# A selective state-space layer with routed experts on one core: state product, state-out product and turned decay sums at other places in the engines' queues

## The chip, the cores and the metric

One core of one Trainium2 chip. The metric is the device time of one execution in microseconds. Before: median 832.32 of 3 runs (832.04 to 833.04).

## The reference, cut to what matters

The input is 16 sequences of 512 tokens with 128 features, float32. Two layers follow one another, each with a residual and a layer norm.

```
# layer 1, for each sequence (4 heads of 64, 128 states)
z, xBC, dt = split(x @ Win.T)                 # 256, 512, 4 columns
xBC = silu(causal_conv4(xBC) + conv_b)        # x_ssm 256, B 128, C 128
dtp = softplus(dt + dt_bias); dA = exp(dtp * A)
h_t = dA_t * h_(t-1) + (dtp_t x_t) B_t        # per head
y_t = C_t . h_t + D x_t
x = layernorm(x + (rmsnorm(y) * norm_w * silu(z)) @ Wout.T)
# layer 2: 8 experts, the 2 best by sigmoid gate for each token
x = layernorm(x + sum of gate * (gelu(x @ W1[e] + b1[e]) @ W2[e] + b2[e]))
```

## The kernel before, in words

The recurrence is computed by chunks of 128 tokens, four to a sequence. Inside a chunk it is a masked matrix: exponents of differences of running sums (`exponents`, line 408, bank `pl`), exponentiated by ACT (`exp_exponents`, 681, into `L`), multiplied with the inner products of B and C by DVE (`mask_chunk`, 973, tile `M`), and applied to the inputs `Xdt` on PE (line 535, bank `p7`). Across chunks it is a state of 128 x 256: the **state product** B^T Xdd (line 549, bank `p6`, right half) gives what a chunk adds; DVE copies it (line 1102) or adds the decayed old state (1105) into `state`; PE multiplies C with the state (the **state-out product**, line 517, `p6`, left half); DVE scales that to `carried` (1075); PE adds it to `p7` (541); DVE adds the skip part to get `yv` (1097); ACT squares it (`square`, 779). POOL makes `Xdd` from `Xdt` (`decay_x`, 1351), `decayed` from `state` (`decay_state`, 1346), and the gated product (`gate_y`, 1329). `Xdt` itself is made by DVE (1069) out of PE's transposes (511, 513) in bank `p5`, after ACT has copied the transposed B out of the same bank to `Btok` (797).

Every engine has a queue written out by hand. The loop over slots (`slots`, 308) has in slot s three sequences at work: sequence s is scanned (`s`), sequence s+1 is projected (`q`), sequence s-1 is normalised and routed (`r`); DVE and POOL finish the ranks and scatters of sequence s-2. A slot has four chunks c = 0 to 3 on PE, ACT and DVE, and a part behind them. In chunk c the projection of block c of the next sequence runs as well: a product (`project_block`, 388, bank `pj`), tap 0 on ACT (`tap0`, 722), taps 1 to 3 on DVE (`tap`, 910; those of block c-1 stand in chunk c, tap 1 at its head and taps 2 and 3 ahead of `yv`; those of block 3 behind the chunks). After the chunks PE runs `z_block` 0 (396), which waits until the taps of blocks 0, 1 and 2 are done because it writes the bank of block 2, then the sums of squares (584, waiting for all four squares), the output product (592), `inner_products` (483) and `z_block` 1.

In chunk 1 PE also turns the split running sums of the next sequence (`turn_parts`, 404, bank `p4`), ACT copies them to `S` (`keep_parts`, 716) for the next slot's exponents, and, behind four normalisations (`rowA`, 805), PE transposes the normalised rows (559) into the same bank `p4`. The bank also holds the ranks of sequence s-2 until DVE has read them (`take_ranks`, 983, at the end of chunk 0, ending with `next_row`, 990). So `turn_parts` has a wait ahead of it:

```
if route:
    wait(pe, rank_read, r.n)      # r.n = s - 1: the ranks that DVE reads in this slot
turn_parts(q, p4[0:KS, 0:P])
```

The order of PE in chunk c is: exponents of c+1, transposes of c, state-out product of c, projection block c, (chunk 1: `turn_parts`), masked product and `carried` of c, state product of c, (chunk 1: 559; chunk 2: gate logits, 574). The order of DVE is: tap 1, `Xdt`, (chunk 0: statistics), `carried`, (chunk 1: `shift`), `mask_chunk` of c+1, taps 2 and 3, `yv`, `state`, (chunk 0: ranks; chunk 1: `place_rows`, 993). Slot 0 has no `route` part and splits the decay sums of all further sequences; slot 15 has no `project` part. After slot 16 a table of tiles is made, the experts run over 136 tiles of rows, and a last loop adds and normalises.

## Time and profile before

| | |
|---|---|
| Median of 3 runs | 832.32 us |
| The profiled execution's own time | 836.54 us |
| Its span, first to last instruction | 834.7 us |
| Mean granted TensorE clock | 0.934 |
| Entering all sequences | 0 to about 55 us |
| Slots 0 to 15 | about 55 to 464 us |
| One slot of 2 to 14 | 25.6 us |

Busy time is given by engine (PE matmuls, PEld weight loads, DVE, ACT, POOL), times from the span's start. In a timeline a line stands for neighbouring instructions of one source line; matmuls are pipelined, so that a row's start is the issue of the first and its duration runs to the modelled end of the last, and rows may overlap. In brackets stands the idle time of the engine before the row, and what ended it. PEclk 1.00 is a granted clock of 2.4 GHz, half of it 1.2 GHz.

### The profile page before, as it was taken

The page shows a single profiled execution, that of the slowest core. Times are in us where ns is not written, and L with a number is a line of the kernel's source. Part 1 is how long each engine was busy: PE and PEld are TensorE (multiplying, and loading weights), DVE is VectorE, ACT ScalarE, POOL GpSimd, SP SyncE. Part 2 cuts the span into 40 slices and gives each one's busy share as a digit, 9 for nine tenths or more (in the row PEclk, how much of TensorE's full clock was granted, in tenths as well). Part 3 has the DMA queues.
Part 4 walks back from the last instruction along what each step waited for, and adds up shares of the span by engine and source line. Part 5 has one row for each costly group of instructions (what it writes and reads, how often), then busy time and mean ns, then how long its engine had stood idle before and what let it go on. Part 6 is the DMA issues. An engine that isn't in the chain of part 4 may idle for free.

```text
span 834.7 us, 21104 instructions
## 1 busy us (share of the span) xinstructions
PE 678.3 (81%) x5092; PEld 552.6 (66%) x5093; DVE 623.1 (75%) x2142; ACT 475.0 (57%) x1179; POOL 435.5 (52%) x498
## 2 busy tenths in 40 slices
PE   6859998998888998889987319999999999989300
PEld 4736565666556665656665309999999999989300
DVE  3457898999999899998996455667667666657485
ACT  2535667676676666676765106555555555546265
POOL 3002345755656656566656653555555555545464
PEclk9979999999999999999999759999999999999755
DMA  9070001110111101111100122222222222222397
GB/s 253 1 252 1 14 17 36 39 36 17 33 33 39 39 17 37 30 36 39 29 24 21 36 74 55 65 67 64 63 62 68 64 61 66 66 57 65 104 297 210
DMA packets 74801, 54.09 MB, mean 65 GB/s; under 512 B 9435, under 2 KB 70110, under 8 KB 74480
## 3 DMA queue, kind: packets, MB, share of 16 engines
q1 hardware_dynamic: 56400, 31.90, 14.5%
q0 software_dynamic: 8448, 16.93, 6.1%
q10 hardware_dynamic: 9888, 4.49, 1.9%
q8 instruction: 29, 0.48, 0.2%
q14 instruction: 36, 0.29, 0.1%
HBM read 31.11 MB, written 22.69 MB: 64 GB/s over the span
## 4 chain that ended last, share of the span: by engine, by line
PE 68%; issue 9%; ACT 8%; DVE 8%; POOL 3%; DMA 2%; ACTq 1%; SPq 1%; DVEq 0%; POOLq 0%
PE pl L628 15%; PE p L640 14%; PE pj L393 4%; PE p L535 3%; PE p L584 3%; PE p L592 3%; PE p L541 2%; PE pj L622 2%; ACT rowA L805 2%; ACT sz L869 2%; POOL sorted_rows L1341 2%; PE p L549 2%; PE p L517 2%; PE pl L419 2%; PE pl L414 2%
## 5 line engine op out<-in xcount | busy, mean ns | idle before, releaser
L848 ACT ACTIVATE L<-pl,b_sb 128x128 f32<-128x128 f32 x544 | 154.9, 368 | 121.7 <-PE pl L628 117.0
L1403 POOL DMA_INDIRECT moe_rows<-yv,xs x136 | 147.3, 1083 | 142.1 <-issue 92.9
L628 PE MATMUL pl<-Btok,M 128*128 128x128 f32 x1088 | 152.5, 284 | 2.4 <-DVE M L1198 2.2
L917 DVE SCALAR_TENSOR_TENSOR acc<-pj,conv_w_sb,acc 128x511 f32<-128x511 f32 (+2 forms) x192 | 142.8, 744 | 4.6 <-ACT acc L725 1.7
L640 PE MATMUL p<-w,L 128*128 x1088 | 144.8, 276 | 1.3 <-ACT L L848 1.3
L628 PEld LDWEIGHTS pl<-Btok,M 128*128 128x128 f32 x1088 | 134.4, 194 | 5.8 <-DVE M L1198 2.5
L640 PEld LDWEIGHTS p<-w,L 128*128 128x128 f32 x1088 | 133.2, 193 | 1.8 <-issue 1.8
L1194 DVE COPY Btok<-pj 128x128 f32<-128x128 f32 x136 | 39.7, 292 | 78.3 <-PE pl L628 63.8
L1354 POOL TENSOR_TENSOR Xdd<-Xdt,cur 128x256 f32<-128x256 f32 x48 | 29.6, 616 | 102.7 <-DVE Xdt L1069 94.4
L1341 POOL DMA_INDIRECT sorted_rows<-rowA,slot x64 | 64.7, 1011 | 19.2 <-issue 17.1
L1341 POOL DMA_INDIRECT sorted_rows<-rowB,slot x64 | 62.7, 979 | 18.0 <-issue 18.0
L393 PE MATMUL pj<-xT,w_xbc 128*128 128x512 f32 x128 | 69.4, 627 | 1.4 <-DVE acc L917 1.4
L725 ACT ACTIVATE acc<-pj,conv_b_sb,conv_w_sb 128x512 f32<-128x512 f32 x64 | 49.3, 772 | 31.7 <-PE pj L393 31.7
L535 PEld LDWEIGHTS p<-M,Xdt 128*64 128x64 f32 x512 | 27.7, 138 | 57.5 <-issue 44.9
L683 ACT ACTIVATE pl<-pl 128x512 f32<-128x512 f32 x64 | 37.3, 582 | 43.5 <-PE pl L419 42.8
L622 PE MATMUL pj<-ident,xs 128*128 128x128 f32 x136 | 40.1, 295 | 23.3 <-DMA xs<-sorted_rows 20.8
L1198 DVE COPY M<-w 128x512 f32 x136 | 56.9, 419 | 0.0
L1334 POOL TENSOR_TENSOR gt<-yv,sz 128x256 f32<-128x256 f32 x64 | 46.9, 733 | 13.5 <-DVE yv L1097 12.8
L535 PE MATMUL p<-M,Xdt 128*64 128x128 f32 x512 | 42.8, 287 | 13.6 <-DVE Xdt L1069 11.4
L1207 DVE TENSOR_TENSOR yv<-p,b2e_mem 128x128 f32<-128x128 f32 x136 | 39.6, 291 | 18.5 <-PE p L640 9.8
L1210 DVE SCALAR_TENSOR_TENSOR yv<-yv,xs 128x128 f32<-128x128 f32 x136 | 47.9, 352 | 4.8
L979 DVE TENSOR_TENSOR M<-pl,Gm 128x512 f32<-128x512 f32 x64 | 43.8, 685 | 0.6
(205 smaller groups left out, 1355.2 us busy)
## 6 DMA issues: line engine op xcount, KB each, us to landing
xs<-sorted_rows SPq DMA_DIRECT2D x136, 65.0 KB
xres<-in_x SPq DMA_DIRECT2D x16, 256.0 KB
w<-in_w SPq DMA_DIRECT2D x2, 2048.0 KB, 9.8
acc<-moe_rows SPq DMA_DIRECT2D x16, 256.0 KB, 4.1
xc<-moe_rows SPq DMA_DIRECT2D x16, 256.0 KB, 4.9
out<-sz ACTq DMA_DIRECT2D x16, 256.0 KB, 4.8
moe_rows<-yv,xs POOLq DMA_INDIRECT x136
xc<-in_x SPq DMA_DIRECT2D x4, 256.0 KB, 4.7
```

The costliest lines, as they stand in the source:

```text
L393: pe.matmul(pj[k % 2][:, :], w_xbc[:, k * P:(k + 1) * P], xT[:, q.n, :], start=True, stop=True).then_inc(proj_psum, 1)
L535: mm = pe.matmul(p7[half, (h // 2) * P:(h // 2 + 1) * P], Xdt[c % 2][:, h * HD:(h + 1) * HD], M[c % 2][:, h, :], start=(h < 2), stop=(c == ...
L622: pe.transpose(pj[k % 2][:, 0:P], xs[k][:, 0:P], ident[:, :]).then_inc(sT_psum, 1)
L628: mm = pe.matmul(pl[k % 2][:, f * P:(f + 1) * P], w1e[k % 2][:, f * P:(f + 1) * P], sT[k % 2][:, :], start=True, stop=True)
L640: mm = pe.matmul(o[:, 0:P], hT[k % 2][:, f, :], w2[:, bass.ds(e, 1), f, :].rearrange("p e d -> p (e d)"), start=(f == 0), stop=(f == FB - 1))
L725: act.activation(acc[:, c, :], pj[c % 2][:, :], ACT.Identity, bias=conv_b[:, c:c + 1], scale=conv_w[:, c, TAPS - 1:TAPS]).then_inc(tap0_do ...
L848: act.activation(hT[k % 2][:, f, :], pl[k % 2][:, f * P:(f + 1) * P], ACT.Gelu, bias=b1[:, bass.ds(e * FB + f, 1)]).then_inc(hT_ready, 1)
L917: ins = dve.scalar_tensor_tensor(out=acc[:, k, j:TOKS], in0=pj[k % 2][:, 0:TOKS - j], scalar=conv_w[:, k, TAPS - 1 - j:TAPS - j], in1=acc[ ...
L1198: dve.tensor_copy(w1e[k % 2], w1[:, bass.ds(e, 1), :].rearrange("p e f -> p (e f)")).then_inc(w1e_ready, 1)
L1210: dve.scalar_tensor_tensor(out=ye[k % 4], in0=ye[k % 4], scalar=xs[k][:, P + 1:P + 2], in1=xs[k][:, 0:P], op0=ALU.mult, op1=ALU.add).then_ ...
L1341: pool.indirect_dma_start(out=sorted_rows[:, :], out_offset=bass.IndirectOffsetOnAxis(slot[q.par][:, c, k:k + 1], 0), in_=(rowA, rowB)[k][ ...
L1403: pool.indirect_dma_start(out=moe_rows[:, :], out_offset=bass.IndirectOffsetOnAxis(xs[k][:, P:P + 1].bitcast(I32), 0), in_=ye[k % 4], in_o ...
```

## The change

On PE the state product of chunk c-1 no longer closes chunk c-1 but stands in chunk c behind the exponents of c+1 and the transposes of c. The state-out product of c stands behind projection block c instead of ahead of it. `turn_parts`, with its waits, stands behind the exponents of chunk 1, ahead of the transposes. On ACT the copy to `S` stands at the head of chunk 1, ahead of the copy to `Btok`, and `set_current` stands in chunk 3. On DVE `state` of c-1 stands behind `Xdt` of c, and `carried` behind `mask_chunk` of c+1. On POOL `decay_x` of chunks 1 and 2 stands ahead of `decay_state` of the same chunk.

```diff
--- before.py
+++ after.py
@@ -502,6 +502,13 @@
                         if not route and c == 0:
                             pe.wait_ge(v_ready, 2)
                         exponents(s if c + 1 < NC else q, (c + 1) % NC)
+                    if project and c == 1:
+                        if q.n == G0:
+                            pe.wait_ge(parts_ready, 2)
+                            pe.wait_ge(decays_ready, 3)
+                        if route:
+                            wait(pe, rank_read, r.n)
+                        turn_parts(q, p4[0:KS, 0:P])
                     if scan:
                         pe.wait_ge(Xdt_ready, n) if not isinstance(n, int) or n > 0 else None
                         wait(pe, Btok_ready, (NC - 1) * s.n + c)
@@ -512,19 +519,20 @@
                         if c + 1 < NC:
                             mm = pe.transpose(p5[:, CC * P:(CC + 1) * P], xc[s.par][:, CC, tok], ident[:, :])
                         mm.then_inc(tr_psum, 1)
-                        if c > 0:
-                            pe.wait_ge(state_ready, (NC - 1) * s.n + c)
-                            pe.matmul(p6[:, 0:DI], xc[s.par][:, CC + 1, tok], state[(c - 1) % 2][:, :],
-                                      start=True, stop=True).then_inc(off_psum, 1)
+                    if scan and c > 0:
+                        k = c - 1
+                        pe.wait_ge(Btok_ready, (NC - 1) * s.n + c)
+                        pe.wait_ge(Xdd_ready, (NC - 1) * s.n + c)
+                        if k == 0:
+                            pe.wait_ge(sz_ready, CC * (s.n + 1))
+                        pe.matmul(p6[:, DI:2 * DI], Btok[k % 2][:, :], Xdd[k % 2][:, :],
+                                  start=True, stop=True).then_inc(state_psum, 1)
                     if project:
                         project_block(q, c)
-                    if project and c == 1:
-                        if q.n == G0:
-                            pe.wait_ge(parts_ready, 2)
-                            pe.wait_ge(decays_ready, 3)
-                        if route:
-                            wait(pe, rank_read, r.n)
-                        turn_parts(q, p4[0:KS, 0:P])
+                    if scan and c > 0:
+                        pe.wait_ge(state_ready, (NC - 1) * s.n + c)
+                        pe.matmul(p6[:, 0:DI], xc[s.par][:, CC + 1, tok], state[(c - 1) % 2][:, :],
+                                  start=True, stop=True).then_inc(off_psum, 1)
                     if scan:
                         pe.wait_ge(M_ready, n + 1)
                         pe.wait_ge(Xdt_ready, n + 1)
@@ -541,13 +549,6 @@
                                 mm = pe.matmul(p7[:, k * P:(k + 1) * P], carried[:, k * P:(k + 1) * P],
                                                ident[:, :], start=False, stop=True, skip_group_check=True)
                         mm.then_inc(y_psum, 1)
-                        if c + 1 < NC:
-                            pe.wait_ge(Btok_ready, (NC - 1) * s.n + c + 1)
-                            pe.wait_ge(Xdd_ready, (NC - 1) * s.n + c + 1)
-                            if c == 0:
-                                pe.wait_ge(sz_ready, CC * (s.n + 1))
-                            pe.matmul(p6[:, DI:2 * DI], Btok[c % 2][:, :], Xdd[c % 2][:, :],
-                                      start=True, stop=True).then_inc(state_psum, 1)
                     if route and c == 1:
                         pe.wait_ge(u_ready, NC * (r.n + 1))
                         wait(pe, rank_read, r.n)
@@ -791,6 +792,8 @@
                     n = NC * s.n + c
                     if scan and c > 0 and (c + 1 < NC or project):
                         exp_exponents(n + 1, c + 1)
+                    if project and c == 1:
+                        keep_parts(q, p4[0:KS, 0:P])
                     if scan and c + 1 < NC:
                         act.wait_ge(tr_psum, n + 1)
                         wait(act, state_psum, (NC - 1) * s.n + c - 1)
@@ -806,15 +809,14 @@
                                            bias=shift[:, k:k + 1], scale=rstd[:, k:k + 1]).then_inc(u_ready, 1)
                     if project:
                         tap0(q, c)
-                    if project and c == 1:
-                        set_current(q)
-                        keep_parts(q, p4[0:KS, 0:P])
                     if not route and c == 2:
                         decay(2, G0, SEQS, 2, 4)
                     if not route and c == 3:
                         decay(3, G0, SEQS, 4, 5)
                     if scan and c > 0:
                         square(s, c - 1)
+                    if project and c == 3:
+                        set_current(q)
                     if route and c == 1:
                         act.wait_ge(u_ready, NC * (r.n + 1))
                         act.wait_ge(uT_psum, r.n + 1)
@@ -1071,10 +1073,14 @@
                     if route and c == 0:
                         statistics(r)
                     if scan and c > 0:
-                        dve.wait_ge(off_psum, (NC - 1) * s.n + c)
-                        dve.tensor_tensor(heads(carried[:, :]), heads(p6[:, 0:DI]),
-                                          per_head(cur[s.par][:, 2, :], c),
-                                          ALU.mult).then_inc(carried_ready, 1)
+                        k = c - 1
+                        dve.wait_ge(state_psum, (NC - 1) * s.n + c)
+                        if k == 0:
+                            dve.tensor_copy(state[0][:, :], p6[:, DI:2 * DI]).then_inc(state_ready, 1)
+                        else:
+                            dve.wait_ge(decayed_ready, (NC - 2) * s.n + k)
+                            dve.tensor_tensor(state[k % 2][:, :], p6[:, DI:2 * DI], decayed[:, :],
+                                              ALU.add).then_inc(state_ready, 1)
                     if route and c == 1:
 
                         dve.wait_ge(rstd_ready, r.n + 1)
@@ -1083,6 +1089,11 @@
                                                  op1=ALU.mult).then_inc(shift_ready, 1)
                     if scan and c + 1 < NC:
                         mask_chunk(s, c + 1)
+                    if scan and c > 0:
+                        dve.wait_ge(off_psum, (NC - 1) * s.n + c)
+                        dve.tensor_tensor(heads(carried[:, :]), heads(p6[:, 0:DI]),
+                                          per_head(cur[s.par][:, 2, :], c),
+                                          ALU.mult).then_inc(carried_ready, 1)
                     if not route and c == 2:
                         split(1, G0, SEQS)
                     if project and c > 0:
@@ -1096,14 +1107,6 @@
                         wait(dve, g_ready, n - 1)
                         dve.tensor_tensor(yv[c % 2][:, :, :], p7[:, 0:DI].rearrange("p (k d) -> p k d", k=CC),
                                           xD[s.par][:, :, c * P:(c + 1) * P], ALU.add).then_inc(yv_ready, 1)
-                    if scan and c + 1 < NC:
-                        dve.wait_ge(state_psum, (NC - 1) * s.n + c + 1)
-                        if c == 0:
-                            dve.tensor_copy(state[0][:, :], p6[:, DI:2 * DI]).then_inc(state_ready, 1)
-                        else:
-                            dve.wait_ge(decayed_ready, (NC - 2) * s.n + c)
-                            dve.tensor_tensor(state[c % 2][:, :], p6[:, DI:2 * DI], decayed[:, :],
-                                              ALU.add).then_inc(state_ready, 1)
                     if c == 0 and not (isinstance(s.n, int) and s.n < 2):
                         take_ranks(s.plus(-2))
                     if c == 1 and not (isinstance(s.n, int) and s.n < 2):
@@ -1368,11 +1371,11 @@
                     pool.wait_ge(ve_ready, r.n + 1)
                     pool.tensor_tensor(rstd[:, :], ve[:, :], neg_half[:, :], ALU.pow).then_inc(rstd_ready, 1)
                 if scan:
+                    decay_x(s, 1)
                     decay_state(s, 1)
-                    decay_x(s, 1)
                     gate_y(s, 0)
+                    decay_x(s, 2)
                     decay_state(s, 2)
-                    decay_x(s, 2)
                     gate_y(s, 1)
                 if scatters:
                     scatter(old, 0, 0)
```

## Rows read from the trace of the kernel before

**Rows 1.** Windows of 25.6 us: slots 7 and 15.
```profile
core 0: us, PE busy (x) PEld busy (x) DVE busy (x) ACT busy (x) POOL busy (x), PEclk, DMA share, GB/s
...
236.40:262.00 25.60, 22.70 (x162) 15.85 (x161) 23.03 (x75) 17.50 (x35) 15.87 (x20) 1.00 0.11 32
...
441.20:466.80 25.60, 17.75 (x134) 13.29 (x131) 16.32 (x74) 8.31 (x19) 17.32 (x21) 0.93 0.08 25
```

**Rows 2.** Timeline of PE, slot 7, chunks 0 to 2 (start, duration, line, shapes, idle).
```profile
238.16 0.66 PE L535 MATMUL p<-M,Xdt 128*64 128x128 f32 x8 [0.18 <-DVE Xdt L1069]
240.06 0.67 PE L549 MATMUL p<-Xdd,Btok 128*128 128x256 f32 x2 [1.24 <-issue]
240.56 0.38 PE L414 MATMUL pl<-too_early,ident_b 128*128 128x512 bf16 x1
...
241.22 0.39 PE L511 MATMUL p<-ident,xc 128*128 128x128 f32 x2
...
241.99 1.02 PE L393 MATMUL pj<-xT,w_xbc 128*128 128x512 f32 x2
242.84 0.22 PE L406 MATMUL p<-ident_b,parts 128*96 128x128 bf16 x1
...
246.21 0.63 PE L559 MATMUL p<-ident,rowA 128*128 128x128 f32 x4 [1.48 <-ACT S L720]
```

**Rows 3.** Timeline of DVE, slot 7, chunks 0 to 2.
```profile
240.14 0.42 DVE L1097 TENSOR_TENSOR yv<-p,xD 128x256 f32<-128x256 f32 x1
240.76 0.42 DVE L1102 COPY state<-p 128x256 f32<-128x256 f32 x1 [0.20 <-PE p L549]
...
241.39 0.17 DVE L990 TENSOR_TENSOR next_row<-p,next_row 128x8 f32<-128x8 f32 x1
...
242.27 0.43 DVE L1069 TENSOR_TENSOR Xdt<-p,cur 128x256 f32<-128x256 f32 x1
...
242.94 0.46 DVE L1081 SCALAR_TENSOR_TENSOR shift<-mv,rstd 128x4 f32<-128x4 f32 x1
...
245.37 0.42 DVE L1097 TENSOR_TENSOR yv<-p,xD 128x256 f32<-128x256 f32 x1
...
247.23 0.74 DVE L917 SCALAR_TENSOR_TENSOR acc<-pj,conv_w_sb,acc 128x511 f32<-128x511 f32 x1
248.39 0.42 DVE L1069 TENSOR_TENSOR Xdt<-p,cur 128x256 f32<-128x256 f32 x1 [0.41 <-issue]
```

**Rows 4.** Timeline of ACT, slot 7, chunk 1.
```profile
241.91 0.27 ACT L797 COPY Btok<-p 128x128 f32<-128x128 f32 x1
243.44 1.65 ACT L805 ACTIVATE rowA<-rowA,shift,rstd 128x128 f32<-128x128 f32 x4 [1.26 <-DVE shift L1081]
...
245.81 0.26 ACT L720 CAST S<-p 96x128 bf16<-96x128 f32 x1
```

**Rows 5.** Timeline of PE, slot 7, chunk 3 and the start of what follows.
```profile
252.14 0.39 PE L511 MATMUL p<-ident,xc 128*128 128x128 f32 x2
...
252.80 1.02 PE L393 MATMUL pj<-xT,w_xbc 128*128 128x512 f32 x2
...
254.92 1.12 PE L401 MATMUL pj<-xT,w_z 128*128 128x512 f32 x2
256.01 2.02 PE L584 MATMUL p<-ones,ysq 128*128 128x96 f32 x16
```

**Rows 6.** Timeline of DVE, slot 7, chunk 3.
```profile
253.00 0.42 DVE L1075 TENSOR_TENSOR carried<-p,cur 128x256 f32<-128x256 f32 x1
253.34 1.52 DVE L917 SCALAR_TENSOR_TENSOR acc<-pj,conv_w_sb,acc 128x510 f32<-128x510 f32 x2
```

**Rows 7.** Timeline of PE: slot 0 (chunk 3), slot 1 (chunk 1), slot 15 (behind chunk 0).
```profile
74.17 1.91 PE L393 MATMUL pj<-xT,w_xbc 128*128 128x512 f32 x2
...
93.15 0.63 PE L559 MATMUL p<-ident,rowA 128*128 128x128 f32 x4 [1.12 <-issue]
...
444.92 1.03 PE L549 MATMUL p<-Xdd,Btok 128*128 128x256 f32 x2 [1.24 <-issue]
```

## The prediction

> **What bounds the kernel now.** I read first the windows, one per slot. The slots 2 to 14 are alike: 25.6 us, in slot 7 PE busy for 22.70 and DVE for 23.03 [rows 1]. Neither engine is full, both are nearly so, and a change of order can cost on one what it gives on the other. The second view is PE's timeline of slot 7. It shows two real holes: 1.24 us ahead of the state product, and 1.48 ahead of the transposes of the normalised rows, ended by ACT's copy to S [rows 2]. These are what the change aims at. With 0.18 ahead of the masked product they make up the 2.9 us that PE is idle. The third view is DVE's timeline: it hardly pauses; it waits 0.41 ahead of the third Xdt [rows 3]. The last is the fourth chunk on both: the z product (254.92) starts as soon as taps 2 and 3 of block 2 end (253.34 + 1.52 = 254.86) [rows 5, 6]. That place has no slack.
>
> **Chunk 0 into 1: the first hole stays, under another name.** I go through slot 7 at its own times. Until the masked product at 238.16 nothing differs. PE then has the exponents at once (0.66, from 240.56 to the transposes at 241.22), done near 239.4. But next comes `turn_parts` with its wait for `rank_read`. DVE gives that at the end of chunk 0, with `next_row`, and its queue up to there is bound by its own work: yv at 240.14. Before, `next_row` came 0.63 behind the start of the state copy (240.76 to 241.39) [rows 3]; that copy is gone from there and yv (of the same duration) stands in its place, so `next_row` starts at 240.77 and ends at 240.94. PE turns the parts at 241.05, 0.11 behind it (S ends at 246.07 and its waiter starts at 246.21, 0.14 behind) [rows 2, 4]. The transposes of chunk 1 come 0.1 later, at 241.15, where they were at 241.22. So PE waits about 1.5 us at `turn_parts` instead of 1.24 at the state product. On ACT, exponents and S copy now lie ahead and done, so Btok follows the transposes at 241.75 instead of 241.91 [rows 4], and Xdt comes at 242.11 instead of 242.27. The state copy stands where `carried` stood, both 0.42, so `shift` comes at 242.79 and the row normalisation at 243.29, 0.15 sooner.
>
> **The second hole closes.** The transposes of the rows no longer wait for S, only for the rows: 243.29 + 1.65 + 0.14 = 245.08, against 246.21 [rows 2, 4]: 1.13 sooner.
>
> **But carried and the taps behind it come later.** The state-out product now stands behind the projection (0.85, 241.99 to 242.84) [rows 2] and waits for the state copy, ready at 242.87: it starts at 243.0 and ends at 243.6. DVE works from Xdt to yv without a pause, 3.10 us before (242.27 to 245.37) and 0.33 more with the state copy among it: yv comes at 242.11 + 3.43 = 245.54, 0.17 later [rows 3]. Carried, with taps 2 and 3 behind it (some 1.77), starts at 243.77 and just doesn't wait. The state add behind yv (0.33) is gone, so the next tap 1 comes 1.53 behind yv (1.86 before, 245.37 to 247.23), at 247.07, and the third Xdt at 247.87, since Btok is there before it: 0.52 sooner than 248.39 [rows 3]. In chunk 2 the state add ends at 248.63; PE has finished projection 2 at 247.83 and waits 0.9 for it: a new hole. State-out at 248.75, carried 0.64 behind it at 249.39, yv at 251.17 (before, 251.09). The gate logits and exponents behind it end at X = 252.02 instead of 252.14 [rows 5]. So of 1.13 us only 0.12 reach the fourth chunk.
>
> **Chunk 3: the price.** Before, from X: carried at X + 0.86, then the taps of block 2 (0.34 behind, 1.52 long), and the z product at X + 2.78 [rows 5, 6]. Now a state product (0.44) and the projection (0.85) are ahead of the state-out product. The 0.44 is read so: three transposes and one state-out product take 0.77 (241.22 to 241.99), two and one take 0.66 (252.14 to 252.80), so a transpose takes 0.11 and a 128x256 product 0.44 [rows 2, 5]. DVE has nothing to do in place of the wait, since the taps 2 and 3 are queued behind carried. Carried comes at X + 0.86 + 0.44 + 0.85 = X + 2.15, the taps end at X + 2.15 + 0.34 + 1.52 = X + 4.01, the z product starts at X + 4.13: 256.15, 1.23 later. The sums of squares started 1.09 behind it, since they waited for the last square; now the square is done in time and they start 0.87 behind it: 257.02 against 256.01. From there to the end of the slot PE works without a hole (z, squares, output, inner products), and everything moves by **1.01 us a slot**. What else moved is covered: `set_current` (0.25) on ACT lies in that engine's free time in chunk 3; POOL gets Xdt sooner than it can use it, and Xdd (0.61) is wanted by nobody until the next chunk. No DMA is added.
>
> **Sum.** Slots 2 to 14: 13 x 1.01 = +13.1. Slot 1 has no ranks to wait for: `turn_parts` runs at once, and by the same count the rows' transposes come at 91.93, right behind carried, instead of 93.15 [rows 7], 1.22 sooner; no `place_rows` is ahead of the third Xdt either, so more of it lasts, some 0.76 at the fourth chunk, and the tail takes 1.13: +0.4. Slot 0 runs partly at half clock (a projection of 1.91 us against 1.02) [rows 2, 7] and starts its second chunk's exponents a cold state product (about 1.0) sooner; I take -1.5, with ends 0 and -3. Slot 15 has no z product and no taps: it loses the 1.24 us wait [rows 7] and its `turn_parts` is absent, so its second chunk gains some 2.5, and chunks 2 and 3 lose 1.0 and 1.1 for the state add between two products of PE: -0.4, ends -2 and +1. Together +11.6. The profiled execution took 836.54 us and would take 848.1; it lies 4.2 above the median of 832.32, so as a median: **844**.
>
> **Rivals.** *A small loss* (13%): DVE's ranks come sooner than I count, or the hole of chunk 2 is smaller, and all slots behave as slot 1: 14 x 0.4 - 1.9 = +3.7, 836. For it: DVE's pauses are inferred from dense rows. Against: yv at 240.14 is queue-bound.
>
> *Faster* (7%): both holes close and the z product has slack after all, because taps 2 and 3 of block 2 don't depend on the chain through the projection. PE would save 1.24 + 1.48 and pay only the 1.29 us by which carried is later: -1.43 a slot, -20 over 14 slots, 812. It decides at the start of the fourth chunk's transposes: from X - 1.1 on the change pays. Against it: `turn_parts` can't pass `rank_read`, and `carried` is ahead of the taps in DVE's queue.
>
> *A clock drop* (13%). In slot 15 PE is idle for 1.04, works 0.66, is idle for 1.24, and the state product then takes 1.03 where it took 0.67 in slot 7: 1.2 GHz instead of 2.4; the slot's mean is 0.93 [rows 2, 1, 7]. The new slot has 0.66 + 0.66 of work, then 1.5 idle, which is a little sparser than slot 7 is now at that place (granted 1.00). If the clock fell there, the projection of chunk 1 would take 0.9 more [rows 2, 7] and the products ahead of it 0.5, all ahead of carried: +1.4 a slot, +18 more over 13 slots, 862. The Trainium skill, TensorE: Matmul & The Clock Gate, Part 1: The HAM clock gate, says that idle stretches put the array at half rate and sustained work brings it back; slots 0 and 15 agree; slot 7's 1.00, with its two holes, shows that holes of this size need not bring it on. By the rule alone the sum would lean to 862, by the rows to 844.
>
> **How the numbers follow.** The forecast has 67%. Its own range is 839 to 850: 0.8 to 1.3 us a slot (10.4 to 16.9) with -4 to +1 for slots 0, 1 and 15. The range is stretched to 835.5 for the small loss and to 851 above; the clock drop and the gain lie outside. A measurement of this kernel tells 0.2%, 1.7 us, from no change. Slower: 67 + 13 + 13, less a little of the small loss that ends within 1.7: 0.89. Same 0.04, faster 0.07.
>
> **What the profile after would show.** Idle of about 1.5 ahead of L406 ended by `next_row` or without a named releaser, none ahead of the state product; the rows' transposes a few tenths behind `carried`, not behind S; idle of 0.9 ahead of the state-out product in chunk 2; DVE idle of about 1 us ahead of carried in chunk 3; PE idle of about 0.7 ahead of the z product. Slots 2 to 14 at 26.6 us. Slots of 25.6 or less would prove me wrong, most likely in the fourth chunk; a granted clock below 1.00 in them would mean the third rival.

## The result and the profile after

| | before | after |
|---|---|---|
| Median | 832.18 us (4 runs) | 837.59 us (4 runs) |
| Ratio, 95% interval | | 1.0068, 1.0051 to 1.0086 |
| The profiled execution's own time, its span | 836.54, 834.7 | 837.40, 835.6 |
| Slot 0, from Gm to Gm | 28.31 | 27.02 |
| Slot 2 | 25.45 | 26.44 |
| Slots 4 to 13, median | 25.61 | 26.02 |
| Slot 14 | 25.61 | 27.73 |

The change makes the kernel slower by 0.68%, 5.4 us, where 11.7 were forecast. The profiled executions differ by less, since the one of before spent 2.7 us more on the entry of the sequences (its first Gm starts at 55.08, the one of after at 52.36) and lay 4.4 above its median. Between the first and the last Gm the kernel after takes 391.7 us and the kernel before 385.3. Behind the last Gm it is 2.7 shorter (391.6 against 394.3). Slot 15 accounts for 1.1 of that; the rest, and the shorter entry, can't be laid to the change, since over all profiles below the part ahead of the first Gm lasts 52.3 to 56.5 us (the kernel after alone: 52.4 to 56.5) and the part behind the last one 387.8 to 395.2. Slot lengths here and below are differences of the starts of Gm, DVE's first instruction of a slot. "Slots of" a length gives the median of slots 4 to 13, without slots of lowered clock. One execution of 2365.23 us, among the six with the small moves back, is slow and stands outside its run's ratio.

The waits of the kernel after, over the whole span (engine and line waiting, releaser: us in total, times, longest):

```profile
PEld p L534 <- DVE state L1082: 29.9, 32, 1.6
...
PEld p L406 <- DVE next_row L992: 20.2, 13, 1.9
...
DVE carried L1094 <- PE p L534: 18.9, 34, 1.2
```

In the kernel before, the same three waits come to 0.8, 3.9 (without a named releaser) and 0.3 us in all. PE waits for the state add ahead of the state-out product (534), for the ranks ahead of the turned parts (406), 13 times, and DVE waits for the state-out product ahead of `carried`. The waits of [rows 2], 1.24 for the state product and 1.48 for S, are gone. PE's timeline of slot 7, from the first exponents, shows where each is:

```profile
234.66 0.38 PE L414 MATMUL pl<-too_early,ident_b 128*128 128x512 bf16 x1
...
239.54 0.26 PE L406 MATMUL p<-ident_b,parts 128*96 128x128 bf16 x1 [1.35 <-DVE next_row L992]
...
243.43 0.65 PE L560 MATMUL p<-ident,rowA 128*128 128x128 f32 x4
...
246.90 0.70 PE L534 MATMUL p<-state,xc 128*128 128x256 f32 x2 [0.54 <-DVE state L1082]
...
250.19 0.39 PE L518 MATMUL p<-ident,xc 128*128 128x128 f32 x2
...
254.26 1.13 PE L401 MATMUL pj<-xT,w_z 128*128 128x512 f32 x2 [0.73 <-DVE acc L919]
...
260.68 0.38 PE L414 MATMUL pl<-too_early,ident_b 128*128 128x512 bf16 x1
```

The holes stand where they were foretold: 1.35 ahead of the parts (foretold 1.5), 0.54 in chunk 2 (0.9), 0.73 ahead of the z product (0.7), and the rows' transposes (L560) come without a wait. DVE in the same slot:

```profile
239.32 0.17 DVE L992 TENSOR_TENSOR next_row<-p,next_row 128x8 f32<-128x8 f32 x1
239.40 0.74 DVE L919 SCALAR_TENSOR_TENSOR acc<-pj,conv_w_sb,acc 128x511 f32<-128x511 f32 x1
240.55 0.42 DVE L1071 TENSOR_TENSOR Xdt<-p,cur 128x256 f32<-128x256 f32 x1 [0.41 <-PE p L520]
...
243.98 0.41 DVE L1108 TENSOR_TENSOR yv<-p,xD 128x256 f32<-128x256 f32 x1
...
245.44 0.74 DVE L919 SCALAR_TENSOR_TENSOR acc<-pj,conv_w_sb,acc 128x511 f32<-128x511 f32 x1
246.10 0.41 DVE L1071 TENSOR_TENSOR Xdt<-p,cur 128x256 f32<-128x256 f32 x1
...
252.34 0.42 DVE L1094 TENSOR_TENSOR carried<-p,cur 128x256 f32<-128x256 f32 x1 [0.86 <-PE p L534]
```

To set the slots side by side I need the start of slot 7 before, one tap and the start of the next slot. Those rows of the kernel before, which did not stand above:

```profile
235.97 0.38 PE L414 MATMUL pl<-too_early,ident_b 128*128 128x512 bf16 x1
...
261.57 0.38 PE L414 MATMUL pl<-too_early,ident_b 128*128 128x512 bf16 x1
```
```profile
241.47 0.74 DVE L917 SCALAR_TENSOR_TENSOR acc<-pj,conv_w_sb,acc 128x511 f32<-128x511 f32 x1
```

The slots are taken here from first exponents to first exponents, which for slot 7 is 0.23 us less than by Gm in both kernels.

| Slot 7, us | before | after | change | foretold |
|---|---|---|---|---|
| start to X (fourth chunk's transposes) | 16.17 | 15.53 | -0.64 | -0.12 |
| X to the z product | 2.78 | 4.07 | +1.29 | +1.35 |
| z product to the next start | 6.65 | 6.42 | -0.23 | -0.22 |
| sum | 25.60 | 26.02 | +0.42 | +1.01 |

Two of three terms are right to 0.06 us, the last of them by luck: from the z product to the sums of squares it is 0.12 us less (0.97 for 1.09), where 0.22 was foretold, and 0.11 more goes behind them (5.45 for 5.56), where nothing was. The first term is not right, and it is half a microsecond in each of 13 slots.

Slot 14 is another matter. The windows of slots 7 and 14 of the kernel after (busy by engine, PEclk, DMA share, GB/s):

```profile
234.17:260.42 26.25, 23.47 (x163) 15.95 (x162) 23.00 (x76) 17.45 (x35) 15.78 (x19) 1.00 0.11 32
...
416.30:444.03 27.73, 24.36 (x163) 16.87 (x162) 23.27 (x76) 17.58 (x35) 15.81 (x19) 0.94 0.10 30
```

The granted clock of TensorE is 0.94 in slot 14: part of it runs at 1.2 GHz instead of 2.4. PE's timeline there:

```profile
422.08 0.34 PE L406 MATMUL p<-ident_b,parts 128*96 128x128 bf16 x1 [1.76 <-DVE next_row L992]
...
423.71 1.87 PE L393 MATMUL pj<-xT,w_xbc 128*128 128x512 f32 x2
```

Behind the hole at the turned parts, 1.76 here, the projection takes 1.87 us instead of 1.02. This was my rival of a clock drop, at the very place, but in one slot of 13. The clock is not all of the 1.7 us by which slot 14 is longer: the hole itself is 0.41 longer than in the others, since DVE gets through its statistics late. DVE idles and takes 0.40 for the add of epsilon, which takes 0.17 in the other slots:

```profile
420.05 0.25 DVE L1034 BATCH_NORM_AGGREGATE mv<-st 128x2 f32<-128x6 f32 x2 [0.17 <-issue]
420.33 0.40 DVE L1037 TENSOR_SCALAR ve<-mv 128x4 f32<-128x4 f32 x1
```

The kernel before has the same delay in its slot 14, and the slot is no longer for it (25.61):

```profile
418.53 0.25 DVE L1032 BATCH_NORM_AGGREGATE mv<-st 128x2 f32<-128x6 f32 x2 [0.16 <-issue]
418.81 0.43 DVE L1035 TENSOR_SCALAR ve<-mv 128x4 f32<-128x4 f32 x1
```

### The profile page after: what moved, and what is told of

Its sections match the earlier page's. It is cut to its first block, busy times and chain, and to the rows that moved or that the text cites. A ratio compares the mean times of both kernels' runs of the same rounds, so it can differ in the third digit from the quotient of the medians.

```text
span 835.6 us, 21104 instructions
## 1 busy us (share of the span) xinstructions
PE 681.0 (82%) x5092; PEld 551.7 (66%) x5093; DVE 621.3 (74%) x2142; ACT 473.9 (57%) x1179; POOL 435.0 (52%) x498
## 4 chain that ended last, share of the span: by engine, by line
PE 62%; DVE 13%; issue 9%; ACT 8%; POOL 3%; DMA 2%; SPq 1%; ACTq 1%; DVEq 0%; POOLq 0%
PE pl L629 15%; PE p L641 14%; PE p L585 3%; PE p L593 3%; DVE acc L919 3%; PE p L534 2%; PE pj L393 2%; PE pj L623 2%; PE pj L401 2%; POOL sorted_rows L1344 2%; ACT rowA L808 2%; ACT sz L871 2%; PE p L575 2%; PE p L401 2%; PE p L489 1%
## 5 line engine op out<-in xcount | busy, mean ns | idle before, releaser
L1344 POOL DMA_INDIRECT sorted_rows<-rowA,slot x64 | 64.7, 1011 | 19.1 <-issue 17.0
L393 PE MATMUL pj<-xT,w_xbc 128*128 128x512 f32 x128 | 67.5, 611 | 1.4 <-DVE acc L919 1.4
L543 PE MATMUL p<-M,Xdt 128*64 128x128 f32 x512 | 42.6, 287 | 11.7 <-DVE Xdt L1071 10.3
L534 PEld LDWEIGHTS p<-state,xc 128*128 128x128 f32 x96 | 15.9, 193 | 43.6 <-DVE state L1082 29.9
```

The source lines that it names most:

```text
L393: pe.matmul(pj[k % 2][:, :], w_xbc[:, k * P:(k + 1) * P], xT[:, q.n, :], start=True, stop=True).then_inc(proj_psum, 1)
L543: mm = pe.matmul(p7[half, (h // 2) * P:(h // 2 + 1) * P], Xdt[c % 2][:, h * HD:(h + 1) * HD], M[c % 2][:, h, :], start=(h < 2), stop=(c == ...
L1344: pool.indirect_dma_start(out=sorted_rows[:, :], out_offset=bass.IndirectOffsetOnAxis(slot[q.par][:, c, k:k + 1], 0), in_=(rowA, rowB)[k][ ...
```

## The experiments

The runs were made on several chips, each beside runs of the kernel before on its own chip, so that ratios are compared, and slot lengths by the profiles.

**The two halves of the change.** First, on the kernel before, the parts alone:

```diff
                         exponents(s if c + 1 < NC else q, (c + 1) % NC)
+                    if project and c == 1:
...
+                        turn_parts(q, p4[0:KS, 0:P])
...
                         project_block(q, c)
-                    if project and c == 1:
...
-                        turn_parts(q, p4[0:KS, 0:P])
...
                         exp_exponents(n + 1, c + 1)
+                    if project and c == 1:
+                        keep_parts(q, p4[0:KS, 0:P])
...
                         tap0(q, c)
-                    if project and c == 1:
-                        set_current(q)
-                        keep_parts(q, p4[0:KS, 0:P])
...
                         square(s, c - 1)
+                    if project and c == 3:
+                        set_current(q)
```

> The kernel before, with the turned parts and the copy to S at the head of chunk 1 and nothing else moved. My theory: the state product still waits for Xdd, the parts then wait some 0.45 us for the ranks, Xdt of chunk 1 comes 0.45 later, the rows' transposes 0.5 sooner, and the third Xdt about where it was: 0 to -0.15 us a slot, 830.5 to 832.5. Rival (the loss comes from the parts' wait for the ranks): +0.4 a slot, 837.

Measured: 0.9949 (0.9934 to 0.9963), 827.05 against 832.23; slots 4 to 13 at 25.30. It is faster by 0.5%, clear of the interval, and by 0.31 a slot, twice what I allowed. The parts wait only 0.23 for the ranks there, because the state product's own wait is ahead of it:

```profile
234.94 0.67 PE L549 MATMUL p<-Xdd,Btok 128*128 128x256 f32 x2 [1.31 <-issue]
...
236.50 0.26 PE L406 MATMUL p<-ident_b,parts 128*96 128x128 bf16 x1 [0.23 <-DVE next_row L991]
```

Then the kernel after, with the parts back behind the projection:

```diff
                         exponents(s if c + 1 < NC else q, (c + 1) % NC)
-                    if project and c == 1:
...
-                        turn_parts(q, p4[0:KS, 0:P])
...
                         project_block(q, c)
+                    if project and c == 1:
...
+                        turn_parts(q, p4[0:KS, 0:P])
...
-                    if project and c == 1:
-                        keep_parts(q, p4[0:KS, 0:P])
...
                         tap0(q, c)
+                    if project and c == 1:
+                        set_current(q)
+                        keep_parts(q, p4[0:KS, 0:P])
...
-                    if project and c == 3:
-                        set_current(q)
```

> The kernel after, with the turned parts behind the projection and the copies on ACT back where they were before; only the state part of the change is left. My theory: the price is made in chunk 3 by the state product, state add, state-out and carried in one chain, so slots stay at +0.3 to +0.5 us: 836 to 838. Rival (the parts' wait for the ranks is the loss): 832 or below.

Measured: 1.0079 (1.0060 to 1.0097), slots of 26.08. The loss is that of the state half, and the rival (the ranks' wait) falls. The two halves alone make -0.31 and +0.47, 0.16 together, but combined 0.41: of the 0.31 that the parts win alone, 0.06 (26.08 to 26.02) is left once the state half is in.

**The wait for the ranks.** The kernel after, with the ranks taken in chunk 0 ahead of the mask of chunk 1 and not behind yv:

```diff
+                    if c == 0 and not (isinstance(s.n, int) and s.n < 2):
+                        take_ranks(s.plus(-2))
                     if scan and c + 1 < NC:
                         mask_chunk(s, c + 1)
...
-                    if c == 0 and not (isinstance(s.n, int) and s.n < 2):
-                        take_ranks(s.plus(-2))
```

> The kernel after, with the ranks read by DVE ahead of the mask of chunk 1 instead of behind yv of chunk 0. My theory: the 1.35 us ahead of the turned parts go, but DVE's queue (mask, yv, tap, Xdt) is the bound behind it, so only the 0.4 us that Xdt of chunk 1 waits for its transposes is won: slots of 25.6, 831.5 to 833. If PE's hole is itself on the path, the slots lose up to 1.3 us and the kernel comes to 821.

Measured: 1.0028 (1.0009 to 1.0046), 833.8; slots 25.78, -0.24 each, where I expected -0.4 and at most 833. The hole ahead of L406 shrinks from 1.35 to 0.67, and only a third of that is won, so PE's hole is not itself on the path for its whole length. That DVE's own queue is the bound behind it was argued and fits.

**Which state product costs.** The kernel after, with only the state product of chunk 0 moved; the other two, and the state-out products and `carried` of chunks 2 and 3, stand where the kernel before has them (the hybrid, below). PE's part, then DVE's and POOL's:

```diff
-                    if scan and c > 0:
+                    if scan and c == 1:
                         k = c - 1
...
+                    if scan and c > 1:
+                        pe.wait_ge(state_ready, (NC - 1) * s.n + c)
+                        pe.matmul(p6[:, 0:DI], xc[s.par][:, CC + 1, tok], state[(c - 1) % 2][:, :],
+                                  start=True, stop=True).then_inc(off_psum, 1)
                     if project:
                         project_block(q, c)
-                    if scan and c > 0:
+                    if scan and c == 1:
                         pe.wait_ge(state_ready, (NC - 1) * s.n + c)
...
+                        if 0 < c < NC - 1:
...
+                            pe.matmul(p6[:, DI:2 * DI], Btok[c % 2][:, :], Xdd[c % 2][:, :],
+                                      start=True, stop=True).then_inc(state_psum, 1)
```
```diff
+                    if scan and c > 1:
+                        dve.wait_ge(off_psum, (NC - 1) * s.n + c)
+                        dve.tensor_tensor(heads(carried[:, :]), heads(p6[:, 0:DI]),
...
                         mask_chunk(s, c + 1)
-                    if scan and c > 0:
+                    if scan and c == 1:
                         dve.wait_ge(off_psum, (NC - 1) * s.n + c)
...
+                    if scan and 0 < c < NC - 1:
...
+                        dve.tensor_tensor(state[c % 2][:, :], p6[:, DI:2 * DI], decayed[:, :],
+                                          ALU.add).then_inc(state_ready, 1)
...
-                    decay_x(s, 2)
                     decay_state(s, 2)
+                    decay_x(s, 2)
```

> The kernel after, but only the state product of chunk 0 is moved; the ones of chunks 1 and 2, their state adds, state-out products and carried stand as before. My theory: chunk 1 keeps its gain (third Xdt 0.65 us sooner than before), chunk 3 is as before: -0.65 us a slot, 822 to 825. Rival (the gain of chunk 1 is eaten elsewhere, by DVE or ACT): 830 or more.

Measured: 0.9876 (0.9855 to 0.9896), 821.66. Slots of 24.88, -0.73 against before, a little more than the 0.65 that I expected. Its rival falls. The same with the turned parts, `set_current` and `keep_parts` back where the kernel before has them:

```diff
                         exponents(s if c + 1 < NC else q, (c + 1) % NC)
-                    if project and c == 1:
...
-                        turn_parts(q, p4[0:KS, 0:P])
...
                         project_block(q, c)
+                    if project and c == 1:
...
+                        turn_parts(q, p4[0:KS, 0:P])
```

> Only the state product of chunk 0 moved, the turned parts and the copies on ACT where they were before. If the state product of chunk 0 is the larger gain: slots of 24.9 to 25.1 us, 822 to 826. If the gain needs both parts of the change: about 25.5, 831.

Measured: 0.9846 (0.9830 to 0.9863), 822.68 against 834.68 on its chip; slots of 24.85. So with the state product of chunk 0 moved, the turned parts may stay where they were. And the kernel after with only the last chunk put back (its state product at the end of the third chunk, its state-out product ahead of the projection, DVE's share with them):

```diff
-                    if scan and c > 0:
+                    if scan and 0 < c < NC - 1:
                         k = c - 1
...
+                    if scan and c == NC - 1:
+                        pe.wait_ge(state_ready, (NC - 1) * s.n + c)
...
                     if project:
                         project_block(q, c)
-                    if scan and c > 0:
+                    if scan and 0 < c < NC - 1:
                         pe.wait_ge(state_ready, (NC - 1) * s.n + c)
...
+                        if c == NC - 2:
...
+                            pe.matmul(p6[:, DI:2 * DI], Btok[c % 2][:, :], Xdd[c % 2][:, :],
+                                      start=True, stop=True).then_inc(state_psum, 1)
```

> The kernel after, with the state product, state add, state-out product and carried of the last chunk back where they were before; the ones of chunks 1 and 2 stay moved. My theory (the price of the last chunk is 1.29 us of chain less what it wins, 0.44 of PE and 0.23 at the squares): slots of 25.4 us, 829 to 831. If the last chunk isn't the price: 26.0 a slot.

Measured: 0.9990 (0.9971 to 1.0008), 834.0; slots of 25.52 against 26.05 of the kernel after on the same chip, a gain of 0.53 where I expected 0.6 and 829 to 831. The last chunk costs 0.53, the third 0.64 (25.52 to 24.88), and the second gives 0.73.

**The hybrid with early ranks.** The kernel with the state product of chunk 0 and the parts moved, and the edit of the ranks on top:

```diff
+                    if c == 0 and not (isinstance(s.n, int) and s.n < 2):
+                        take_ranks(s.plus(-2))
                     if scan and c + 1 < NC:
                         mask_chunk(s, c + 1)
...
-                    if c == 0 and not (isinstance(s.n, int) and s.n < 2):
-                        take_ranks(s.plus(-2))
```

> The kernel in which only the state product of chunk 0 is moved, and the ranks are read ahead of the mask of chunk 1. If both gains add (0.65 and 0.4 us a slot): 25.6 - 1.05 = 24.55 us a slot, 817 to 820. If DVE's work of 23.0 us a slot or ACT's chain bounds it first: no better than the one without early ranks.

Measured: 0.9842 (0.9811 to 0.9874), 820.66 against 834.84; slots of 24.75. The gains don't add: 0.13, not 0.4. Its interval overlaps that of the one that moves the state product of chunk 0 alone, so I can't say which is best; both are about 1.5% faster than the kernel before, and faster than the kernel after by more.

**What the last chunk waits for.** Two runs on the kernel after:

```diff
-                    if scan and c > 0:
+                    if scan and 0 < c < NC - 1:
                         dve.wait_ge(off_psum, (NC - 1) * s.n + c)
...
                         tap(q, c - 1, 3)
+                    if scan and c == NC - 1:
+                        dve.wait_ge(off_psum, (NC - 1) * s.n + c)
+                        dve.tensor_tensor(heads(carried[:, :]), heads(p6[:, 0:DI]),
+                                          per_head(cur[s.par][:, 2, :], c),
+                                          ALU.mult).then_inc(carried_ready, 1)
```

> The kernel after, with taps 2 and 3 of block 2 ahead of carried in chunk 3. If the z product waits only for the taps behind carried, as I say, it starts some 0.3 us sooner, as soon as the product with carried is done, and yv comes as late as it did: -0.2 to -0.3 us a slot, 833.5 to 835.5. If the taps aren't what it waits for: 837.6.

Slots of 26.02, as before the edit. The taps were what the z product waited for: its wait is gone, the product with `carried` waits 0.41 instead, and the z product starts 3.66 behind the fourth chunk's transposes and not 4.07. But the sums of squares are sooner by less, since yv and its square stand behind the same chain:

```profile
257.48 0.71 PE L549 MATMUL p<-ident,carried 128*128 128x128 f32 x4 [0.41 <-DVE carried L1105]
258.03 1.02 PE L401 MATMUL pj<-xT,w_z 128*128 128x512 f32 x2
259.16 2.02 PE L585 MATMUL p<-ones,ysq 128*128 128x96 f32 x16
```

From the z product to the sums it is 1.13 here and 0.97 in the kernel after, and from there to the next slot 5.56 and 5.45, so 0.27 of the 0.41 is gone again behind the z product. The rest lies ahead of the fourth chunk (15.6 to 15.7 in most slots, 15.53 in the first profile); the kernel after on two other chips has 15.6 there too. The 0.2 that I expected did not come.

```diff
+                    if scan and c == NC - 1:
+                        pe.wait_ge(state_ready, (NC - 1) * s.n + c)
+                        pe.matmul(p6[:, 0:DI], xc[s.par][:, CC + 1, tok], state[(c - 1) % 2][:, :],
+                                  start=True, stop=True).then_inc(off_psum, 1)
                     if project:
                         project_block(q, c)
-                    if scan and c > 0:
+                    if scan and 0 < c < NC - 1:
                         pe.wait_ge(state_ready, (NC - 1) * s.n + c)
```

> The kernel after, with the state-out product of chunk 3 ahead of projection block 3. By the prediction's sum the projection stands with 0.85 us in the path to carried, so the slot would gain up to 0.85: 827. By the rival chain (state product, state add on DVE, state-out, carried) the state-out product has to wait for the add anyway: -0.14 us a slot, 835.5 to 837, with a hole of 0.6 us on PE ahead of it.

Slots of 26.28, 0.26 longer, both of my numbers missed. The state-out product waits 0.52 for the state add, so `carried` gains only 0.07, and the projection, tap 0 and the square pay for the hole:

```profile
259.44 0.70 PE L532 MATMUL p<-state,xc 128*128 128x256 f32 x2 [0.52 <-DVE state L1086]
259.97 1.02 PE L393 MATMUL pj<-xT,w_xbc 128*128 128x512 f32 x2
```

So the chain state product, state add, state-out, carried makes the last chunk long, and not the projection's 0.85 by itself: with the projection out of the way the add on DVE is late instead. The medians of these two, 845.56 (1.0137, 1.0095 to 1.0179) and 850.85 (1.0179, 1.0146 to 1.0212), say little of the edits: both profiles hold three slots with the granted clock at 0.94, of 27.3 to 28.1 us.

**The clock.** The kernel after again, on another chip:

> The kernel after once more, beside the others on one chip. A control: slots of 26.0 us wherever TensorE's granted clock stays at 1.00; here and there a slot of 27.3 to 27.8 where it falls behind the hole ahead of the turned parts, and a spread of some us between runs from the number of these.

1.0132 (1.0111 to 1.0153), 845.62 against 834.68: twice the loss. Its slots of full clock are 26.05 long, as on the first chip to 0.03; slots 10 and 14 are 27.49 and 27.76 at 0.94. With three products that nothing reads in the hole:

```diff
                         exponents(s if c + 1 < NC else q, (c + 1) % NC)
+                    if scan and project and route and c == 1:
+                        pe.wait_ge(sz_ready, CC * (s.n + 1))
+                        for _ in range(3):
+                            pe.matmul(p6[:, 0:DI], ident[:, :], w_xbc[:, 0:DI], start=True, stop=True)
                     if project and c == 1:
```

> The kernel after, with three products of 128x256 that nothing reads (about 1.3 us of PE work) in the hole ahead of the turned parts. If idle PE there is what takes the clock down, no slot is longer than 26.3 us any more, the granted clock is 1.00 in all slots of 2 to 14, and the median lies 1 to 5 us below the control's though PE does more. If not: as the control, or slower by up to 0.1 us a slot.

1.0084 (1.0054 to 1.0114), 842.29. PE does more, and the median is 3.3 us below the control's; six of its seven executions lie below all six of the control, the seventh above five of them, and the two intervals just touch. The longest of slots 2 to 14 is 26.44, a little more than the 26.3 that I expected (the longer ones are slots 2, 6, 9 and 14), and the clock is 1.00 in all of them. No fall in 13 slots is weak evidence by itself: at the rate of the kernels with the hole, 17 in 104 below, it would come by luck one time in ten. Its slot 14, with six matmul instructions more than the kernel after has there:

```profile
421.04:447.45 26.41, 24.58 (x169) 16.92 (x168) 23.24 (x76) 17.52 (x35) 15.83 (x19) 1.00 0.10 31
```

On a third chip, both kernels and the moves that I costed at nothing:

> The kernel before once more, for a profile on the same chip as the kernel after. If the further loss of the kernel after on some chips comes from falls of TensorE's clock that only it has: slots 2 to 14 at 25.3 to 25.8 us with none above 26.5, ratio 1.000 within 0.2%. If this kernel falls as often: slots of 27 us here too.

0.9995 (0.9977 to 1.0013); slots 25.61, none above 25.84, clock 1.00.

> The kernel after on that chip. Slots of 26.0 us by its order of work alone (+0.41 a slot, about +5 in all), and up to 6 us more by slots of 27.3 to 27.8 and by a longer entry of the sequences, both with a lower granted clock: 1.006 to 1.014 of the kernel before.

1.0139 (1.0114 to 1.0163), 846.05; slots 26.08, and slots 4 and 11 at 27.70 and 27.57. Slot 4:

```profile
162.81 0.26 PE L406 MATMUL p<-ident_b,parts 128*96 128x128 bf16 x1 [1.73 <-DVE next_row L992]
...
163.93 1.91 PE L393 MATMUL pj<-xT,w_xbc 128*128 128x512 f32 x2
```

The kernel after, with `set_current` and the order of chunk 1 and 2 on POOL back:

```diff
                         tap0(q, c)
+                    if project and c == 1:
+                        set_current(q)
...
-                    if project and c == 3:
-                        set_current(q)
...
-                    decay_x(s, 1)
                     decay_state(s, 1)
+                    decay_x(s, 1)
                     gate_y(s, 0)
-                    decay_x(s, 2)
                     decay_state(s, 2)
+                    decay_x(s, 2)
```

> The kernel after, with set_current back in chunk 1 on ACT and POOL's decay_state ahead of decay_x as before. The prediction costs both moves at nothing: slots of 26.0 us within 0.1. If they are on the path: 0.15 us or more longer.

1.0087 (1.0060 to 1.0114), 843.1 (842.75 without the execution of 2365.23); regular slots 25.96, within 0.12 of the kernel after. `set_current` and POOL's order are off the path or cost a tenth at most. That its median is 3 us below the kernel after's isn't explained: its profile has three slots of lowered clock.

Over all profiles, falls of the clock in slots 2 to 14:

| Hole ahead of the turned parts | Profiles | Slots | With a fall |
|---|---|---|---|
| 1.35 to 1.47 (the kernel after three times, small moves back, chunk 3 back, hybrid, taps first, state-out first) | 8 | 87 | 7 |
| 1.71 to 1.84, the same kernels | 8 | 17 | 10 |
| at most 0.86, none, or filled (state alone, early ranks, hybrid with ranks, state product of chunk 0 alone, filler) | 5 | 65 | 0 |
| the kernel before twice: 1.20 to 1.27 at the state product, 1.48 to 1.54 at the rows' transposes | 2 | 26 | 0 |
| parts alone: 1.31 at the state product, 0.23 at the parts (1.07 in slot 2) | 1 | 13 | 1 |

In all 18 falls it is the projection of chunk 1 that takes 1.80 to 1.92 us. The longer the hole at the parts, the likelier the fall: 7 of 87 against 10 of 17. At the rate of the shorter ones, 7 in 87, no fall in the 65 slots of the third row would come by luck one time in 200. The kernel before has a hole as long, 1.48 ahead of the rows' transposes, and no fall in 26 slots; that would come by luck one time in nine, so whether the place of a hole counts beside its length is open.

What makes a hole 1.71 instead of 1.35 can be read from the traces, and is not chance alone. DVE's add of epsilon and POOL's `Xdd` of chunk 0 start within a tenth of a microsecond of each other in most slots. In slot 13 of the first profile of the kernel after, the add starts first:

```profile
394.04 0.17 DVE L1037 TENSOR_SCALAR ve<-mv 128x4 f32<-128x4 f32 x1
394.06 0.63 POOL L1357 TENSOR_TENSOR Xdd<-Xdt,cur 128x256 f32<-128x256 f32 x1
```

In slot 4 of the third chip's profile POOL does:

```profile
160.79 0.63 POOL L1357 TENSOR_TENSOR Xdd<-Xdt,cur 128x256 f32<-128x256 f32 x1
160.81 0.65 DVE L1037 TENSOR_SCALAR ve<-mv 128x4 f32<-128x4 f32 x1
```

Over the 16 profiles the add is long (0.37 to 0.66 us instead of 0.17) in 34 of 208 slots. In all 34 it starts 0 to 0.29 behind the start of `Xdd` and ends 0.03 to 0.05 behind its end; in none of the other 174 does it start more than 0.01 behind the start of `Xdd` and before its end. So the add is held until POOL's product ends, whenever POOL is first. In slot 14 POOL is first in every profile, and 6 of the 8 kernels with the hole at the parts fall there. No run moved one of the two instructions.

## Why the prediction was right and wrong

**The sign and the places were right.** The wait ahead of the state product came back as a wait for the ranks, the rows' transposes stopped waiting for S, and the gain of the second chunk was lost in the third and the fourth. Shown: PE's and DVE's rows above, and the last chunk and the third put back one by one (0.53 and 0.64 a slot).

**The rival that came nearest was the small loss** (13%, 836). It named ranks that come sooner than I count and a smaller hole in chunk 2, at 0.4 a slot. The ranks came 0.14 sooner against the first exponents, the hole is 0.54 and not 0.9, and the slots lost 0.42. Against it I had put that yv at 240.14 is bound by DVE's queue; it came 0.13 sooner.

**The size was wrong in one term: "X = 252.02 instead of 252.14".** X came 0.64 sooner, not 0.12. No single wait was missed. The sum up to X was a chain of spacings read off the kernel before as if its instructions stood back to back, and at least one held a small wait. The largest: I took 0.80 from the head of a tap 1 to Xdt (241.47 to 242.27 in [rows 3] and the row above). In the kernel after the same two stand at 245.44 and 246.10: 0.66. Before, Xdt was waiting for Btok, in a pause too short to be marked: the copy of Btok ended at 242.18 (241.91 + 0.27 in [rows 4]), 0.09 ahead of it. The others: from the first exponents to yv of chunk 0, 4.04 for 4.17; the ranks to the parts and to Xdt, 1.23 for 1.34; yv to the next tap, 1.46 for 1.53; and some 0.06 more from there on. All have one sign; that the others held a wait too is inferred and not shown. The state add of chunk 2 came sooner with the third Xdt, so the hole there is smaller too. Thirteen slots of 0.59 make -7.7 us. Slots 1 and 15 took 0.4 and 0.7 less than foretold, slot 0 0.2 more, slot 2 0.6 more than a regular one, and slot 14 1.7 more: together 6.3 us less than forecast, as the median.

**The parts alone** failed by the same habit. I had the third Xdt "about where it was"; it came sooner, as tap and Xdt stood 0.66 apart, and the slots won 0.31.

**Chunk 3** was right as a number (+1.35, measured +1.29) but its working was half the truth. "Carried comes at X + 0.86 + 0.44 + 0.85" came out at X + 2.15, exactly. But the state-out product had a second reason to wait, the state add, nearly as late as the projection; so moving the projection out of the way gains nothing, as its own run shows.

**The other slots.** Slot 0: -1.3 (foretold -1.5). Slot 1: 0.0 (+0.4). Slot 2: +1.0 as foretold, by luck, since the slots behind it show +0.4. Slot 15 and what follows up to the sums of squares: 19.1 to 18.0, -1.1 (foretold -0.4).

**The clock drop** got 13% as a state of all slots, 862. It is real, at the place and for the price named (foretold 1.4; 27.49 against 26.05 in a slot whose hole is 1.40), but it comes in one to three slots of 13 and differs by run. I treated it as yes or no. On the first chip's profile it is some 1.3 of the loss, and 0.4 is DVE's delay in slot 14; on the others the kernel after lost 11 us where regular slots explain some 5. The rest there is falls, with the longer holes ahead of some of them (about 3 in the profiles), and a remainder that no profile shows: on both chips the profiled run was the fastest of its six (844.53 of 845.62, 841.04 of 846.05). The median 844 would have fitted those chips, but for a wrong reason. The Trainium skill, TensorE: Matmul & The Clock Gate, Part 1: The HAM clock gate, has the array go to half rate after idle stretches and come back with sustained work. The falls behind the hole, and none where it was shortened or filled, agree in kind. That a hole of 1.35 us is followed by a fall now and then, and one of 1.7 more often than not, the table above shows and I had not inferred it.

## What to carry to other kernels

Before you add up spacings of a queue that you expect to run sooner, take each from a place where the two instructions are back to back for certain (elsewhere in the same trace), since pauses of a tenth hide in rows that overlap; here they all biased the forecast the same way. When a product is moved to close a hole, move the one that has the hole and no other: here three state products were moved for one, and the one alone wins 1.5% where three lose 0.7% or more. And a hole that takes another name need not be neutral: look at the granted clock by stage and in more than one profile. When one small instruction is long in some slots only, look at what the other engines had just started.

## What was not expected of the hardware

The same kernel with the same slots (26.02 to 26.08) was 0.7% behind the kernel before on one chip and 1.3 to 1.4% on two others. The fall of the clock behind a given hole is in part a matter of chance: of the 104 holes of 1.35 to 1.84 us 17 were followed by one, 7 of the 87 up to 1.47 and 10 of the 17 from 1.71 on. With the hole filled by useless products no slot fell and the median was 3.3 us lower, though the intervals just touch. And a tiny DVE instruction, the add of epsilon (line 1037), takes up to 0.66 us instead of 0.17 whenever POOL's `Xdd` has started ahead of it, be it by 0.02 us; in slot 4 of the third chip's profile this lengthened the hole at the parts from 1.35 to 1.73. In the kernel before the same delay, in slots 4, 10 and 14, cost nothing (slots of 25.6).
